# Self attention of a perceiver layer: stacks made by DMA, maxima from high parts, layer norms by row tile

## Chip, core and metric

The kernel runs on one core of one Trainium2 chip. The metric is device time in microseconds: 1697.44 us, the median of three runs (1695.24 to 1698.91).

## What is computed

The layer is cross attention, then self attention with a sparse mixing, then a mixture of experts. Only the self attention is touched. `x` has 512 rows of 512 features, 16 heads of 32 features.

```python
Q = split_heads(jnp.einsum('bsd,od->bso', x, W_Q))
K = split_heads(jnp.einsum('bsd,od->bso', x, W_K))
V = split_heads(jnp.einsum('bsd,od->bso', x, W_V))
Q = layernorm(Q, q_ln_w, q_ln_b)      # over the 32 features of a head
K = layernorm(K, k_ln_w, k_ln_b)
scores = jnp.einsum('bhqd,bhkd->bhqk', Q, K) / jnp.sqrt(jnp.float32(hd))
attn = jax.nn.softmax(scores, axis=-1)
context = jnp.einsum('bhqk,bhkd->bhqd', attn, V)
...
v_weights = sparse_W_V.mean(axis=2)
o_weights = sparse_W_O.mean(axis=1)
```

## The kernel before

All of the program is a sequence of blocks. In a block each engine runs its own list of instructions in order, synchronised by semaphores that are written out by hand, and a block begins on every engine when the one before has ended. The change touches the two blocks `self_projections` and `self_attend`. Constants: `P` 128, `D` and `N` 512, `NT` = `DC` = `G` = `HG` = 4 (row tiles, contraction chunks, groups of heads, heads of a group), `H` 16, `HD` 32, `STK` = `MROW` = 96.

Scores need more precision than one pass gives, so a query or key is held as a high part (rounded to fp32r) and a low part (the rest). A stack has 96 rows a head: for the queries high, high, low, for the keys high, low, high. One matmul over 96 rows then is the sum of three products. `c.stacks` holds the queries, `c.skst` the keys. Two more rows (96 and 97) of `c.stacks` hold the negated row maximum in two parts, against ones in `c.skst`, so that the matmul of 98 rows yields shifted scores for the exponential.

`self_projections`, by engine:

- TensorE (`project`, line 1001) makes all four row tiles of the raw queries in one set of PSUM banks, then all of the keys, each tile being four fp32 matmuls (eight records in the trace). `turn` (L1013) transposes the normalised tiles. The value products come last and reuse the banks of the keys.
- VectorE first sums the mixing weights (L1074, L1076), then centres (L1046 to L1050), sums the squares (L1054), scales (L1058), always over four tiles at once (128x2048), splits into high and low (L1068, L1070) and copies the high part to one place of the stack (L512).
- ScalarE squares (L1102), takes the root (L1106), applies the affine part of the layer norm out of PSUM (L1114), copies the low part to one place (L510) and the values to SBUF (L1123).
- SyncE issues four DMAs a stack for the third place (L508). One call of `stack_copies` is four operations, one for each head of a group, of 32 partitions by 2048 elements (256 KB).
- GpSimd fills the rows of ones and builds the mixing matrices.

`self_attend`: TensorE makes for head after head and row tile after row tile the scores of a query tile against all keys (`whole`, L1190) in one of two PSUM banks, VectorE takes their maximum over the row (L1278), and `whole(i)` waits for the maximum of `i - 2`. After four tiles VectorE negates and splits the maxima (L1282 to L1285), TensorE turns them into rows (`turn`, L1200), ScalarE copies these into the stack (L1249). This runs 20 tiles (`LEAD`) ahead. Then the loop: `scores` (L1208) makes transposed scores in one of three banks, ScalarE takes the exponential (L1258), and after four of them `weighted` adds values (L1219) and denominators (L1223) into the banks `o` and `den`. These two banks are shared by all groups: at the first round of a group TensorE waits for `s_out`, that is for VectorE's `normalise` of the group before (a reciprocal, L1271, and a product, L1273), which VectorE does behind the maxima of a head:

```python
                if h % HG == 2 and h // HG >= 2:
                    normalise(h // HG - 2)
```

The block after, `sparse_mix`, reads all of the normalised result `c.aoT`.

Of the kernel before, what the change touches and what calls it, by code (L numbers as in the profile page):

```python
# [20 lines left out]
P = 128  # L21
# [932 lines left out]
def self_projections(nc, c):  # L954


    with ExitStack() as stack:
        sb, pb, sem = allocators(nc, stack, "sp")
        vm = sb("vm", [P, H])
        om = sb("om", [P, HD])  # L960
        total = sb("total", [P, NT * H])
        mean = sb("mean", [P, NT * H])
        spread = sb("spread", [P, NT * H])
        std = sb("std", [P, NT * H])
        rstd = sb("rstd", [P, NT * H])
        cen = sb("cen", [P, NT, D])
        nrm = sb("nrm", [P, NT, D])
        full = sb("full", [P, G, N])
        hi = sb("hi", [P, G, N], F32R)
        lo = sb("lo", [P, G, N], F32R)  # L970
        queries = pb("queries", [P, NT, D])
        keys = pb("keys", [P, NT, D])
        turned = queries[:, :, :]
        s_raw, s_cen, s_sq, s_var, s_std, s_nrm, s_tp, s_full, s_hi, s_lo, s_v, s_val, s_ones = (
            sem(n) for n in ("raw", "cen", "sq", "var", "std", "nrm", "tp", "full", "hi", "lo", "v", "val", "ones"))
        s_copy_act, s_copy_dve, s_copy_dma = sem("copy_act"), sem("copy_dve"), sem("copy_dma")
        s_step = sem("step")
        s_vm, s_om, s_bv, s_bo = (sem(n) for n in ("vm", "om", "bv", "bo"))
# [3 lines left out]
        KINDS = ((c.stacks, 1, 2, 0), (c.skst, 2, 1, 2))  # L982

        def heads(ap):
            return ap.rearrange("p t (h d) -> p (t h) d", d=HD)

        def wide(ap):
            return ap[:, :].unsqueeze(2).broadcast_to([P, NT * H, HD])

        @block.sync  # L990
        def _(sp):
            for n, (stacks, second_hi, _, _) in enumerate(KINDS):
                sp.wait_ge(s_hi, G * (n + 1))
                stack_copies(sp, stacks, f32(hi[:, :, :]), second_hi, s_copy_dma)
            sp.wait_ge(s_copy_dma, 16 * 2 * HG)

        @block.tensor
        def _(pe):
            def project(out, w, t):
                for k in range(DC):  # L1000
                    mm = pe.matmul(out[:, t, :], c.hT[:, k, t * P:(t + 1) * P], w[:, k, :],
                                   start=(k == 0), stop=(k == DC - 1))
                return mm

            def turn(n):

                pe.wait_ge(s_nrm, n + 1)
                if n:

                    pe.wait_ge(s_full, G)  # L1010
                for g in range(G):
                    for t in range(NT):
                        mm = pe.transpose(turned[:, g, t * P:(t + 1) * P], nrm[:, t, g * P:(g + 1) * P], c.ident[:, :])  # L1013
                    mm.then_inc(s_tp, 1)

            pe.wait_ge(c.sq_in, 16)
            for t in range(NT):
                mm = project(queries, c.swqT, t)
            mm.then_inc(s_raw, 1)
            pe.wait_ge(c.sk_in, 16)  # L1020
            for t in range(NT):
                mm = project(keys, c.swkT, t)
            mm.then_inc(s_raw, 1)
            turn(0)
            pe.wait_ge(c.sv_in, 16)

            pe.wait_ge(s_cen, 2)
            for t in range(NT):
                if t == NT // 2:
                    turn(1)  # L1030
                project(keys, c.swvT, t).then_inc(s_v, 1)

        @block.vector
        def _(dve):
            steps = 0

            def step(instruction):

                nonlocal steps
                steps += 1  # L1040
                instruction.then_inc(s_step, 1)
                dve.wait_ge(s_step, steps)

            def centre(n, raw):
                dve.wait_ge(s_raw, n + 1)
                step(dve.tensor_reduce(total[:, :], heads(raw[:, :, :]), AX.X, ALU.add))  # L1046
                step(dve.tensor_scalar(mean[:, :], total[:, :], 1.0 / HD, None, ALU.mult))
                if n:
                    dve.wait_ge(s_nrm, n)
                dve.tensor_tensor(heads(cen[:, :, :]), heads(raw[:, :, :]), wide(mean), ALU.subtract).then_inc(s_cen, 1)  # L1050

            def normalise(n):
                dve.wait_ge(s_sq, n + 1)
                step(dve.tensor_reduce(spread[:, :], heads(nrm[:, :, :]), AX.X, ALU.add))  # L1054
                dve.tensor_scalar(std[:, :], spread[:, :], 1.0 / HD, EPS, ALU.mult, ALU.add).then_inc(s_var, 1)
                dve.wait_ge(s_std, n + 1)
                step(dve.reciprocal(rstd[:, :], std[:, :]))
                dve.tensor_tensor(heads(nrm[:, :, :]), heads(cen[:, :, :]), wide(rstd), ALU.mult).then_inc(s_nrm, 1)  # L1058

            def split(n):  # L1060
                if n:

                    dve.wait_ge(s_copy_act, HG)
                    dve.wait_ge(s_copy_dve, HG)
                    dve.wait_ge(s_copy_dma, 16 * HG)
                for g in range(G):
                    dve.wait_ge(s_full, G * n + g + 1)
                    dve.tensor_copy(hi[:, g, :], full[:, g, :]).then_inc(s_hi, 1)  # L1068
                    dve.wait_ge(s_hi, G * n + g + 1)
                    dve.tensor_tensor(lo[:, g, :], full[:, g, :], f32(hi[:, g, :]), ALU.subtract).then_inc(s_lo, 1)  # L1070

            wv, wo = mixing_parts(c)
            dve.wait_ge(c.mix_in, 16 * 5 * HG)
            dve.tensor_reduce(vm[:, :], wv, AX.X, ALU.add).then_inc(s_vm, 1)  # L1074
            for i in range(2):
                dve.tensor_reduce(om[:, HD // 2 * i:HD // 2 * i + HD // 2], wo[i], AX.X, ALU.add).then_inc(s_om, 1)  # L1076
            dve.wait_ge(s_om, 2)
            dve.tensor_scalar(om[:, :], om[:, :], 1.0 / TOPM, None, ALU.mult).then_inc(s_om, 1)
            dve.wait_ge(s_vm, 1)
            dve.wait_ge(s_bv, 1)  # L1080
            for j in range(HG):
                rows = slice(HD * j, HD * j + HD)
                dve.tensor_scalar(c.mix_bv[rows, H * j:H * j + H], vm[rows, :], 1.0 / TOPM, None, ALU.mult).then_inc(s_bv, 1)
            centre(0, queries)
            normalise(0)
            centre(1, keys)
            split(0)
            normalise(1)
            stack_copies(dve, KINDS[0][0], f32(hi[:, :, :]), 0, s_copy_dve)
            split(1)  # L1090
# [842 lines left out]
```

## Time and profile before

| | us |
|---|---|
| median of three runs | 1697.44 |
| the profiled execution | 1702.76 |
| its span | 1701.0 |
| TensorE busy | 1551.6 (91%) |
| VectorE busy | 1197.0 (70%) |
| ScalarE busy | 969.2 (57%) |
| GpSimd busy | 373.7 (22%) |

The two blocks lie between 1177 and 1357 us. A row of the timeline gives start, duration, engine, line, operation, output, inputs, shapes and count of a run of equal instructions, in brackets the idle time of the engine before it and what ended that. Ends of matmuls are modelled, so starts are the better measure on TensorE (PE). The granted clock is a share of 2.4 GHz.

### The profile page before, as it was taken

The numbers are of one execution on the slowest core, as the hardware profiler recorded it, in microseconds if no ns is written. First come the engines' busy times: TensorE is split into PE (matmuls) and PEld (weight loads), VectorE is DVE, ScalarE is ACT, GpSimd is POOL, SyncE is SP. The second block draws the span as 40 slices with busy tenths as digits, with TensorE's granted clock in tenths as the row PEclk, the third lists the DMA queues.
The fourth block names the chain that finished last, engine by engine and source line by source line (L and its number), as shares of the span: only waits on it lengthen the run. The fifth ranks groups of instructions, "written<-read, shape, count | busy, mean of one in ns | idle before, by whom it ended". The sixth has DMA issues, their size and how long they took to land. (4 is left out here: it accounts for less than half of the span.)

```text
span 1701.0 us, 21706 instructions
## 1 busy us (share of the span) xinstructions
PE 1551.6 (91%) x7992; PEld 819.7 (48%) x7992; DVE 1197.0 (70%) x1834; ACT 969.2 (57%) x1167; POOL 373.7 (22%) x141
## 2 busy tenths in 40 slices
PE   6799999999999799999999999998877706899998
PEld 4466666666665333333333333333443203777775
DVE  5777677677677799999999999996866384320002
ACT  3366666666666688888888888881444411111110
POOL 4453654654652105030012001001000000100001
PEclk9899999999999899999999999998968757799999
DMA  4454454453453654565454444443110090379993
GB/s 173 153 194 153 145 187 150 159 186 139 171 185 105 156 125 118 138 172 144 116 137 125 124 116 115 118 99 50 26 25 1 7 395 1 118 275 325 327 330 103
DMA packets 117336, 250.26 MB, mean 147 GB/s; under 512 B 9704, under 2 KB 26088, under 8 KB 112752
## 3 DMA queue, kind: packets, MB, share of 16 engines
q1 hardware_dynamic: 115520, 244.68, 46.0%
q0 software_dynamic: 1280, 4.20, 0.8%
q8 instruction: 64, 1.05, 0.3%
q14 instruction: 40, 0.33, 0.1%
q10 hardware_dynamic: 432, 0.01, 0.0%
HBM read 182.26 MB, written 61.34 MB: 143 GB/s over the span
## 5 line engine op out<-in xcount | busy, mean ns | idle before, releaser
L748 ACT ACTIVATE att_pr<-att_sc 128x1024 f32<-128x1024 f32 x512 | 496.2, 1022 | 75.3 <-PE att_sc L665 75.3
L798 DVE TENSOR_TENSOR att_tot<-att_tot,att_pr 128x2048 f32<-128x2048 f32 x200 | 467.1, 2336 | 22.0 <-ACT att_pr L748 1.8
L491 DVE CUSTOM_DVE_ANT_0 ctx_size<-ctx_tot,ctx_size 128x512 f32<-128x512 f32 x512 | 333.0, 688 | 134.6 <-PE ctx_tot L411 130.9
L462 ACT ACTIVATE ctx_size<-ctx_dif 128x1024 f32<-128x1024 f32 x256 | 262.3, 1025 | 125.7 <-PE ctx_dif L411 125.7
L665 PE MATMUL att_sc<-g_stacks,att_kst 98*128 98x512 f32 x1024 | 309.0, 424 | 1.5 <-DVE g_stacks L589 1.5
L665 PEld LDWEIGHTS att_sc<-g_stacks,att_kst 98*128 98x128 f32 x1024 | 173.9, 189 | 236.7 <-ACT att_pr L748 211.5
L679 PE MATMUL att_o<-att_pr,att_val 128*32 128x512 f32 x2048 | 273.6, 606 | 2.0 <-issue 1.9
L1742 ACT ACTIVATE ex_hidT<-ex_hp,m_b 128x128 f32<-128x128 f32 x120 | 34.3, 368 | 185.2 <-PE ex_hp L1697 185.1
L411 PE MATMUL ctx_dif<-ctx_k_dif,f_q_hi 32*128 32x512 f32 x512 | 129.2, 501 | 10.1 <-DVE ctx_best L491 6.1
L411 PE MATMUL ctx_tot<-ctx_k_sum,f_q_hi 32*128 32x512 f32 x512 | 128.4, 498 | 0.0
L86 PE MATMUL f_proj<-f_wv_hi,g_stacks 128*128 128x512 f32 x320 | 120.8, 420 | 0.0
L86 PE MATMUL f_proj<-g_stacks,f_wk_hi 128*128 128x512 f32 x352 | 119.4, 420 | 0.2 <-DVE f_k_lo L206 0.2
L1697 PEld LDWEIGHTS ex_hp<-ex_xT,m_w 128*128 128x128 f32 x960 | 111.0, 194 | 8.0 <-issue 8.0
L1697 PE MATMUL ex_hp<-ex_xT,m_w 128*128 128x128 f32 x960 | 111.4, 278 | 0.8 <-issue 0.8
L1710 PE MATMUL ex_yp<-m_w,ex_hidT 128*128 128x512 f32 x240 | 105.5, 592 | 0.0
L411 PEld LDWEIGHTS ctx_dif<-ctx_k_dif,f_q_hi 32*128 32x128 f32 x512 | 47.8, 183 | 106.7 <-issue 53.5
L100 POOL TENSOR_TENSOR g_stacks<-f_raw,g_stacks 128x2048 fp32r<-128x2048 f32 x21 | 96.7, 4605 | 1.7
L679 PEld LDWEIGHTS att_o<-att_pr,att_val 128*32 128x32 f32 x2048 | 40.4, 108 | 96.8 <-issue 95.4
L593 POOL TENSOR_TENSOR o_aoT<-att_whole,att_rs 128x512 f32<-128x512 f32 x3 | 9.4, 3139 | 330.2 <-DVE att_rs L805 330.2
L1750 DVE COPY ex_xT<-ex_tx 128x512 f32<-128x512 f32 x15 | 10.4, 692 | 96.0 <-PE ex_tx L1651 90.5
L1756 DVE COPY o_yT<-ex_yp 128x512 f32<-128x512 f32 x15 | 10.4, 690 | 91.4 <-PE ex_yp L1710 91.4
L86 PEld LDWEIGHTS f_proj<-g_stacks,f_wk_hi 128*128 128x128 f32 x352 | 60.2, 189 | 29.2 <-issue 20.1
(269 smaller groups left out, 1974.5 us busy)
## 6 DMA issues: line engine op xcount, KB each, us to landing
m_w<-in_W SPq DMA_DIRECT2D x30, 2048.0 KB, 13.6
att_kst<-keys_scratch SPq DMA_DIRECT2D x192, 256.0 KB, 3.9
f_raw<-in_ctx SPq DMA_DIRECT2D x32, 1024.0 KB, 6.0
keys_scratch<-f_k_hi SPq DMA_DIRECT2D x32, 512.0 KB, 2.8
keys_scratch<-f_k_lo SPq DMA_DIRECT2D x32, 512.0 KB, 3.2
values_scratch<-ctx_v SPq DMA_DIRECT2D x32, 512.0 KB, 3.1
att_val<-values_scratch SPq DMA_DIRECT2D x64, 256.0 KB, 2.6
rows_scratch<-mix_blank SPq DMA_DIRECT2D x1, 3840.0 KB, 26.0
```

What stands on the lines that cost most here:

```text
L86: mm = pe.matmul(out, left, right, start=(n == 0), stop=(n == 3 * len(a) - 1))
L100: pool.tensor_tensor(c.lo[b], raw[:, :, :], f32(c.hi[b]), ALU.subtract).then_inc(c.s_lo, 1)
L411: mm = pe.matmul(out[:, r * CH:(r + 1) * CH], c.q_hi[rows, g, t * P:(t + 1) * P], keys[m % 2][rows, g, :], start=True, stop=True)
L462: act.activation(size[:, i % ABS, :], dif[:, :], ACT.Abs).then_inc(s_size, 1)
L491: dve.tensor_tensor_reduce(out=size[:, i % ABS, r * CH:(r + 1) * CH], in0=tot[i % 2][:, r * CH:(r + 1) * CH], in1=size[:, i % ABS, r * CH: ...
L665: mm = pe.matmul(sc[pair % PAIRS][:, r * N:(r + 1) * N], kst[m % CHUNKS][:, j, at:at + P], c.stacks[0:STK + 2, HG * (T // PER_G) + j, :], ...
L679: mm = pe.matmul(o[at, :], val[m % CHUNKS][:, T % KT, at], pr[:, T % SLOTS, j, :], start=first, stop=False, skip_group_check=True)
L748: act.activation(pr[:, T % SLOTS, 2 * s:2 * s + 2, :], sc[(2 * T + s) % PAIRS][:, :].rearrange("p (j q) -> p j q", j=2), ACT.Exp, scale=SC ...
L798: dve.tensor_tensor(tot[b % 2][:, :, :], so_far, pr[:, T % SLOTS, :, :], ALU.add).then_inc(s_add, 1)
L1697: mm = pe.matmul(hp[tau % 2][:, f, :], w1[b][:, k, f * P:(f + 1) * P], xT[tau % 2][:, k, :], start=(k == 0), stop=(k == DC - 1))
L1710: mm = pe.matmul(yp[tau % 2][:, :], hidT[tau % 2][:, f, :], w2[b][:, f, :], start=(f == 0), stop=(f == FC - 1))
L1742: act.activation(hidT[tau % 2][:, f, :], hp[tau % 2][:, f, :], ACT.Relu, bias=b1[:, f, :]).then_inc(s_hid, 1)
```

## The change

The mixing sums go from VectorE at the head of `self_projections` to GpSimd in `self_attend`, as a chain of halvings (`add_up`). The projections run by row tile: eight PSUM banks take the eight raw tiles, all of the layer norm works on one tile (128x512), and ScalarE writes the high part by one affine operation and the full value by a second; GpSimd subtracts them (VectorE for the last tile). Only the first value tile is made there. All three places of both stacks are filled by DMAs from SyncE, 24 in all, those of the keys issued in the second block. `self_attend` takes the maxima from a product of the high parts alone (32 rows), with one row of shift instead of two. The three other value tiles are made in the lead in twelve pieces, and TensorE waits for all DMAs before the first `scores`. The banks `o` and `den` of a group are copied to SBUF (`take`), TensorE waits for that copy, and the normalising is done in four pieces of 128 columns, one behind the maxima of each later head.

The diff, cut to its core:

```diff
+def add_up(pool, out, src, room, s_add, done):
+    half = src.shape[-1] // 2
+    pool.tensor_tensor(room[:, :, 0:half], src[:, :, 0:half], src[:, :, half:], ALU.add).then_inc(s_add, 1)
+    while half > 1:
+        half, done = half // 2, done + 1
+        pool.wait_ge(s_add, done)
+        dst = room[:, :, 0:half] if half > 1 else out.unsqueeze(2)
+        pool.tensor_tensor(dst, room[:, :, 0:half], room[:, :, half:2 * half], ALU.add).then_inc(s_add, 1)
+    return done + 1
...
 def self_projections(nc, c):
...
+            sp.wait_ge(s_hi, NT)
+            for place in (0, 1):
+                stack_copies(sp, c.stacks, f32(hi[0][:, :, :]), place, c.s_copy)
+            sp.wait_ge(s_lo, NT)
+            stack_copies(sp, c.stacks, f32(lo[0]), 2, c.s_copy)
...
+            for n in range(TILES):
+                if n == NT:
+                    pe.wait_ge(c.sk_in, 16)
+                project(raw[n], c.swkT if n >= NT else c.swqT, n % NT).then_inc(s_raw, 1)
+                if n >= 2:
+                    turn(n - 2)
...
+            project(raw[0], c.swvT, 0).then_inc(s_v, 1)
+            turn(TILES - 2)
+            turn(TILES - 1)
...
+            centre(0)
+            for n in range(1, TILES):
+                spreads(n - 1)
+                centre(n)
+                scale(n - 1)
+            spreads(TILES - 1)
+            scale(TILES - 1)
...
+            for n in range(TILES):
                 if n:
+                    root(n - 1)
+                square(n)
+                if n >= 2:
+                    affine(n - 2)
...
+            for n in range(TILES - 1):
...
+                pool.tensor_tensor(lo[kind][:, :, at], full[:, n % 2, :, :], f32(hi[kind][:, :, at]), ALU.subtract).then_inc(s_lo, 1)
...
 def self_attend(nc, c):
...
+            for place in (0, 2):
+                stack_copies(sp, c.skst, f32(hi[1][:, :, :]), place, c.s_copy)
+            stack_copies(sp, c.skst, f32(lo[1]), 1, c.s_copy)
+            sp.wait_ge(c.s_copy, 16 * 2 * 3 * HG)
...
-                pe.matmul(full[i % 2][:, :], c.stacks[0:STK, h, t * P:(t + 1) * P], c.skst[0:STK, h, :],
+                pe.matmul(full[i % 2][:, :], hi[0][at, g, t * P:(t + 1) * P], hi[1][at, g, :],
                           start=True, stop=True).then_inc(s_full, 1)
...
-                    pe.wait_ge(s_out, g)
+                    pe.wait_ge(s_take, 2 * g)
...
             for i in range(LEAD):
                 whole(i)
...
                 if i % NT == NT - 1 and i > NT:
                     turn(i // NT - 1)
+                if 1 <= i <= DC * (NT - 1):
+                    value_product(i - 1)
+            pe.wait_ge(s_val, NT - 1)
+            pe.wait_ge(c.s_copy, 16 * 2 * 3 * HG)
...
+                dve.reciprocal(rs[:, at], total).then_inc(s_rs, 1)
+                dve.wait_ge(s_rs, PIECES * g + piece + 1)
+                dve.tensor_tensor(c.aoT[:, g, at], values, rs[:, at], ALU.mult).then_inc(s_out, 1)
+
+            def take(g):
+
                 dve.wait_ge(s_pv, NT * (g + 1))
                 if g >= 1:
...
+                for n, bank in enumerate((den, o)):
+                    dve.tensor_copy(held[:, n, :], bank[:, :]).then_inc(s_take, 1)
+
+            later = [(g, piece) for g in range(G) for piece in range(PIECES)]
             for h in range(H):
                 for i in range(NT * h, NT * h + NT):
                     dve.wait_ge(s_full, i + 1)
                     dve.tensor_reduce(c.neg[:, h, i % NT:i % NT + 1], full[i % 2][:, :], AX.X, ALU.max).then_inc(s_max, 1)
+                    if i % STEPS == HG * 2 and i // STEPS >= 2:
+                        take(i // STEPS - 2)
...
+                if h >= 2 * HG + 2:
+                    normalise(*later.pop(0))
+            while later[0][0] < G - 2:
+                normalise(*later.pop(0))
+            take(G - 2)
+            for g, piece in later:
+                normalise(g, piece)
```

## Rows read from the trace of the kernel before

**Rows 1.** windows: span, busy time and count of each engine, PEclk, DMA share, GB/s

```profile
1177.00:1242.00 65.00, 49.95 (x128) 23.18 (x128) 45.41 (x46) 27.23 (x24) 8.89 (x8) 0.87 0.25 46
1242.00:1260.40 18.40, 15.97 (x37) 9.02 (x37) 15.16 (x37) 2.39 (x5) 0.00 (x0) 0.50 0.00 0
1260.40:1352.50 92.10, 78.61 (x411) 33.61 (x411) 44.79 (x83) 43.52 (x77) 0.00 (x0) 0.85 0.00 1
```

**Rows 2.** timeline of TensorE, projections and the first score matmul

```profile
1177.26 16.84 PE L1001 MATMUL sp_queries<-a_swqT,g_hT 128*128 128x512 f32 x32 [1.11 <-PEq L542]
...
1193.93 13.90 PE L1001 MATMUL sp_keys<-a_swkT,g_hT 128*128 128x512 f32 x32
...
1207.66 1.91 PE L1013 MATMUL sp_queries<-g_ident,sp_nrm 128*128 128x128 f32 x16
...
1212.85 8.80 PE L1001 MATMUL sp_keys<-a_swvT,g_hT 128*128 128x512 f32 x16 [3.28 <-DVE sp_cen L1050]
...
1242.29 1.22 PE L1190 MATMUL sa_full<-a_skst,g_stacks 96*128 96x512 f32 x2 [10.82 <-DVE sa_shift L1265]
```

**Rows 3.** groups of VectorE, both blocks: busy, mean ns, idle before

```profile
L1278 DVE TENSOR_REDUCE g_neg<-sa_full 128x1 f32<-128x512 f32 x64 | 41.5, 686 | 26.2 <-PE sa_full L1190 25.7
...
L1271 DVE RECIPROCAL sa_rs<-sa_den 128x512 f32<-128x512 f32 x4 | 13.4, 3354 | 23.1 <-PE sa_den L1223 23.1
...
L1070 DVE TENSOR_TENSOR sp_lo<-sp_full,sp_hi 128x512 fp32r<-128x512 f32 x8 | 5.5, 692 | 0.3
...
L512 DVE CAST a_skst<-sp_hi 32x2048 fp32r<-32x2048 f32 x4 | 4.9, 1214 | 0.1
...
L1282 DVE TENSOR_SCALAR sa_shift_hi<-g_neg 128x4 fp32r<-128x4 f32 x16 | 2.7, 170 | 0.6
```

**Rows 4.** timeline of ScalarE, projections

```profile
1208.36 2.78 ACT L1114 ACTIVATE sp_full<-sp_queries,a_aff 128x512 f32<-128x512 f32 x4 [4.61 <-PE sp_queries L1013]
...
1232.71 7.71 ACT L510 ACTIVATE a_skst<-sp_lo 32x2048 fp32r<-32x2048 f32 x4 [1.53 <-DVE sp_lo L1070]
...
1240.44 1.08 ACT L1123 ACTIVATE a_sval<-sp_keys 128x512 f32<-128x512 f32 x2
```

**Rows 5.** groups of GpSimd, whole span

```profile
L100 POOL TENSOR_TENSOR g_stacks<-f_raw,g_stacks 128x2048 fp32r<-128x2048 f32 x21 | 96.7, 4605 | 1.7
```

**Rows 6.** timelines of GpSimd and VectorE in the context projections

```profile
72.71 4.59 POOL L100 TENSOR_TENSOR f_third<-f_raw,f_third 128x2048 fp32r<-128x2048 f32 x1
...
73.11 4.74 DVE L480 TENSOR_TENSOR ctx_k_dif<-f_k_hi 128x512 fp32r<-128x512 f32 x1
```

**Rows 7.** timeline of SyncE's queue, a stack's four DMAs

```profile
1216.25 3.44 SPq L508 DMA_DIRECT2D g_stacks<-sp_hi  x4
```

**Rows 8.** windows, two microseconds while they move

```profile
1219.00:1221.00 2.00, 2.00 (x6) 0.87 (x5) 1.61 (x4) 1.57 (x2) 0.00 (x0) 1.00 0.96 221
```

**Rows 9.** the tile sp_hi: its DMAs from issue to landing

```profile
DMA to landing us min/median/max: 3.1/4.3/5.4
```

**Rows 10.** timeline of TensorE, rounds of the loop

```profile
1279.06 0.50 PE L1190 MATMUL sa_full<-a_skst,g_stacks 96*128 96x512 f32 x1
...
1283.90 0.50 PE L1190 MATMUL sa_full<-a_skst,g_stacks 96*128 96x512 f32 x1
...
1291.62 1.93 PE L1219 MATMUL sa_o<-sa_pr,a_sval 128*32 128x512 f32 x8 [4.66 <-DVE o_aoT L1273]
...
1295.19 0.70 PE L1190 MATMUL sa_full<-a_skst,g_stacks 96*128 96x512 f32 x1
...
1330.13 0.96 PE L1208 MATMUL sa_sc<-g_stacks,a_skst 98*128 98x512 f32 x3
...
1333.66 0.96 PE L1208 MATMUL sa_sc<-g_stacks,a_skst 98*128 98x512 f32 x3
...
1341.60 2.34 PE L1208 MATMUL sa_sc<-g_stacks,a_skst 98*128 98x512 f32 x4
...
1347.18 0.96 PE L1208 MATMUL sa_sc<-g_stacks,a_skst 98*128 98x512 f32 x3
```

More of the change, by code:

```diff
@@ L954, in self_projections @@
 def self_projections(nc, c):
+    TILES = 2 * NT
     with ExitStack() as stack:
         sb, pb, sem = allocators(nc, stack, "sp")
[L959 to L976, printed above, removed]
@@ L977, in self_projections @@
-        s_step = sem("step")
-        s_vm, s_om, s_bv, s_bo = (sem(n) for n in ("vm", "om", "bv", "bo"))
+        total = sb("total", [P, TILES, H])
+        mean = sb("mean", [P, 2, H])
+        spread = sb("spread", [P, 2, H])
+        std = sb("std", [P, 2, H])
+        rstd = sb("rstd", [P, 2, H])
+        cen = sb("cen", [P, 3, D])
+        sq = sb("sq", [P, D])
+        full = sb("full", [P, 2, G, P])
+        hi, lo = c.own_hi, c.own_lo
+        raw = [pb(f"raw{n}", [P, D]) for n in range(TILES)]
@@ L979, in self_projections @@
+        s_raw, s_total, s_mean, s_cen, s_sq, s_spread, s_var, s_std, s_rstd, s_nrm, s_tp, s_full, s_hi, s_lo, s_v, s_ones = (
+            sem(n) for n in ("raw", "total", "mean", "cen", "sq", "spread", "var", "std", "rstd", "nrm", "tp", "full", "hi",
+                             "lo", "v", "ones"))
+        s_last, s_val = sem("last"), sem("val")
         nc.clear_and_free_semaphores(c.spent)
         block = stack.enter_context(nc.Block())
-        KINDS = ((c.stacks, 1, 2, 0), (c.skst, 2, 1, 2))
@@ L1033, in _ @@
+            pe.wait_ge(c.sv_in, 16)
+            pe.wait_ge(s_hi, 1)
+            pe.wait_ge(s_full, 1)
+            project(raw[0], c.swvT, 0).then_inc(s_v, 1)
+            turn(TILES - 2)
+            turn(TILES - 1)
         @block.vector
         def _(dve):
[L1035 to L1044, printed above, removed]
-                dve.wait_ge(s_raw, n + 1)
[L1046 to L1055, printed above, removed]
-                dve.wait_ge(s_std, n + 1)
[L1057 to L1090, printed above, removed]
-            stack_copies(dve, KINDS[1][0], f32(hi[:, :, :]), 0, s_copy_dve)
@@ new lines, in centre @@
+            def centre(n):
+                dve.wait_ge(s_raw, n + 1)
+                dve.tensor_reduce(total[:, n, :], heads(raw[n][:, :]), AX.X, ALU.add).then_inc(s_total, 1)
+                dve.wait_ge(s_total, n + 1)
+                dve.tensor_scalar(mean[:, n % 2, :], total[:, n, :], 1.0 / HD, None, ALU.mult).then_inc(s_mean, 1)
+                if n >= 3:
+                    dve.wait_ge(s_tp, n - 2)
+                dve.wait_ge(s_mean, n + 1)
+                dve.tensor_tensor(heads(cen[:, n % 3, :]), heads(raw[n][:, :]), wide(mean[:, n % 2, :]),
+                                  ALU.subtract).then_inc(s_cen, 1)
```

239 lines of the change are left out of this document (135 added, 104 removed).

## The prediction, made blind

> **What bounds the kernel now.** The windows view cuts the two self attention blocks into stages [rows 1]: 65.0 us for the projections, 18.4 us for a lead of maxima, 92.1 us for the loop. TensorE is busy for 50.0, 16.0 and 78.6 us of these, so only the loop is TensorE's, and the lead runs at a granted clock of 0.50, the lower of the two levels (1.2 GHz). The timeline of TensorE names the holes. In the projections the query tiles take 16.84 us, the key tiles 13.90 us, sixteen transposes 1.91 us; TensorE waits 3.28 us for VectorE before the values, and sits idle for 10.82 us before the first score matmul at 1242.29 [rows 2]. That hole is VectorE (four copies of 1214 ns after the splits [rows 3]) and ScalarE (four copies in 7.71 us, then two value tiles to 1241.5), which build the stacks [rows 4]. So VectorE and ScalarE in turn set the projection stage, and the work is in blocks of four tiles, so that little overlaps. The lead is set by VectorE's 686 ns maxima [rows 3]. In the loop one round of four scores takes 4.84 us (1279.06 to 1283.90), but the round in which a group of heads ends takes 11.29 us (1283.90 to 1295.19), of which 4.66 us is TensorE's wait for VectorE to normalise [rows 10]. All behind it (sparse mixing, routing, experts) waits for the block to end, so what is saved here comes off the end.
>
> **The change, part by part.** Positions are in the profiled execution of before: span 1701.0 us, measured 1702.76 us, 0.3% over the median of 1697.44. I sum differences and subtract them from the median.
>
> *Projections by row tile.* One projection of a tile is eight matmul records of 13.90/32 = 0.434 us, 3.43 us with overlap. The 16.84 us of the queries is 2.96 us over that, the slow clock at the start, which stays [rows 2]. TensorE then does 8 x 3.43 + 2.96 = 30.4 us and, between them, five turns of four transposes at 1.91/16 = 0.12 us, 0.5 us each: the last raw tile is there at 1177.26 + 33.0 = 1210.2. VectorE does per tile two reductions, two tensor products of 0.69 us (the row of 128x512 [rows 3]) and three small ones of 0.17: 3.4 us with gaps, under TensorE's 3.93. ScalarE does a square and two affines, 2.78/4 = 0.70 us each, and a small root [rows 4]: 2.4 us. GpSimd's low part is a quarter of 4605 ns, 1.15 us [rows 5]. Tail behind 1210.2: VectorE centres the last tile (1.75), scales the one before (0.95), sums the squares (0.9), waits for the root (0.7) and scales (0.95), 5.3 us; turn 0.6; ScalarE still has the affines of tile 6 and a value tile, so its last affine ends at 7.7; the last low part 0.8. That is 8.5 us, 1218.7. V product and turn 6 lie under it. The mixing sums (three reductions) leave VectorE's head of the queue at no gain, since they ended before the first queries were there.
>
> *Who queues behind what.* VectorE now issues in order spreads, centre, scale, with a wait for ScalarE in each; the waiting instruction blocks the next tile's centring, and that blocks ScalarE's square. GpSimd's low part of a tile falls at the start of the next tile but two, where VectorE does its small mean operation. The trace shows such a meeting: VectorE's 128x512 tensor_tensor beside GpSimd's took 4.74 us, starting 0.4 us after it, both ending within 0.6 us of each other [rows 6]. So each meeting can cost up to 1.15 us. VectorE has 0.5 us of slack per tile; I take 1.0 us in all, bounds 0 and 8 x 1.15 = 9 us. Stage end 1219.7, and with 0.8 us between blocks (ScalarE's last value, 1240.44 + 1.08, to 1242.29, as now [rows 2, 4]) the first score matmul at 1220.5. Gain over 1242.29: 21.8 us.
>
> The Trainium skill (SBUF — State Buffer, "Who interferes with whom") says that a VectorE operation with two SBUF inputs, or a copy or tensor_scalar in a two-port mode, and a GpSimd operation exclude each other for the whole instruction. The trace agrees (4.74 us for what alone takes 0.69). The rule speaks against moving the splits and sums to GpSimd. By it every meeting is charged in full, which is the first rival below; the row by itself leaves open whether the small operations meet it.
>
> *Stacks by DMA.* Removed: eight copies on VectorE and eight on ScalarE (4.9 and 7.7 us a stack [rows 3, 4]), which were the hole before 1242.29, already counted. Added: 24 DMAs of 256 KB on SP's queue instead of 8. Four are issued in 3.44 us [rows 7], and at a DMA share of 0.96 the engines move 221 GB/s [rows 8], 1.18 us for 256 KB. Query stacks: first issue when four high parts are ready, near 1203.5, twelve take 14.2 + 1.7 us, to 1219.4. Key stacks start with the second block, 1219.7, end 1235.6. Who waits: TensorE before the first score of the loop, near 1243. Cover 7 us; cost nothing. SP issues nothing else until the expert weights, in the next block.
>
> *The lead.* TensorE no longer waits for stacks. Each of twelve steps has a 32-row matmul (0.21 us for 512 columns at 2.4 GHz; the trace has no 32-row one here, its nearest are three 98-row ones in 0.96 us [rows 10] and two 96-row ones in 1.22 us at half clock [rows 2], the bounds) and one piece of a value product, 0.86 us: 1.07 us, more than VectorE's 0.69, so 12.9 us, two turns 1.0. TensorE's clock: after the 3.28 us gap of before sixteen records took 8.80 instead of 6.87 us [rows 2], 1.9 us lost; the gap here is some 4 us, and I take 2.5 us (bounds 0, and 12.9 if the clock never rises). Then six more steps at 0.72, a turn, the row copy, 6.3 us with the wait. Sum 22.7 us against 18.1 (1242.29 to 1260.40 [rows 1, 2]). First score at 1243.2: gain 17.2 us. The shorter shift (one row for two, one small operation of 170 ns for three) saves VectorE 0.33 us a head, under TensorE. GpSimd's mixing sums: 3 x 2032 elements per partition at 4605/2048 ns [rows 5] is 13.7 us, with overheads 18 us, free until VectorE's first normalisation (some 25 us into the loop). They may hold VectorE's small operation once a head: 0 to 2.3 us each, taken in the bounds.
>
> *The loop.* Its rounds stay as they are: the same number of matmuls, and the pace of the two full banks. What goes is the wait for normalising. Excess now: 6.45 us (11.29 - 4.84) at each of the first two boundaries (the second repeats the first), 4.41 us at the third (7.94, 1333.66 to 1341.60, against 3.53, 1330.13 to 1333.66), and 2.05 us of slow clock in the round behind that (5.58, to 1347.18) [rows 10]: 19.4 us. What comes: two copies of a bank, 0.65 us each (the reduction's row; a copy out of PSUM is of the same shape). The first two pairs stand behind the first maximum of a head, so the maximum after next is 1.3 us late and TensorE's fourth score matmul with it: 1.3 us twice. The third pair lies in VectorE's idle time, under four scores. The normalising pieces (reciprocal 3354/4 = 0.84 us [rows 3] and product 0.2, 1.1 us) go behind each head's maxima: 3.0 + 0.2 + 1.1 = 4.3 us of VectorE in 4.84. Late next is nothing. The slow first round gives back 0.5 us. Loop 92.1 - 19.4 + 2.6 - 0.5 = 74.8 us, a gain of 17.3. The last normalisation in four pieces is 4.7 instead of 4.1 us: +0.6.
>
> *Sum.* 17.2 (projections and lead together) + 17.3 - 0.6 = 33.9 us; 1697.4 - 33.9 = 1663.5.
>
> **Rivals.**
> 1. *VectorE and GpSimd exclude each other.* For: [rows 6]. Against: the two meet only for small operations, with 0.5 us slack. Full price: 8 x 1.15 in the projections, some 3 in the lead: +12, 1675.
> 2. *TensorE's clock stays at 1.2 GHz through the lead.* For: the lead of before has 0.50 throughout [rows 1], with TensorE 16.0 of 18.4 us in use by the modelled ends. Against: value products fill it without gaps, and products of that kind brought the clock up at 1177: 2.96 us lost are seven slow records [rows 2]. Price 12.9 - 2.5 = +10, 1673.
> 3. *Copying the banks out does not take the wait away.* TensorE's values still wait for VectorE behind its maxima; if the copies came behind a whole head (2.6 us) each boundary would keep 4 to 5 us: +9, 1672. Against: they stand behind one maximum in the program.
> 4. *Slower than before: the stacks' DMAs don't overlap.* TensorE waits for all 24 before any score. At 4.3 us (the median landing time now [rows 9]) one behind the other they would end at 1203.5 + 103 = 1307, 64 us behind the lead's end: 1663.5 + 64 = 1727. It decides for slower from (1243.2 + 33.9 - 1203.5)/24 = 3.1 us a DMA. Against: while each took 4.3 us to land, the engines moved 221 GB/s, which is 1.18 us apiece, so they do overlap [rows 8, 9].
> 5. *More than forecast:* no meeting on VectorE, the clock comes back at once, the tail is a microsecond shorter: 1657.
>
> **How the numbers follow.** Forecast 0.62, rival 1 0.12, rival 2 0.09, rival 3 0.04, rival 4 0.03, rival 5 0.10. The forecast's own range is 1659 to 1669 (the turns, the tail and the pace of the lead, each a microsecond or two). For 8 in 10 with the bounds of both unknown costs I reach to rival 5 below, and above to where rivals 1 to 3 hold in full: 1655 to 1675. Under 0.2% (3.4 us) can't be told from no change; only rival 4, cut short, would end there. Faster 0.96, same 0.01, slower 0.03.
>
> **What would show it.** The first 32-row score matmul some 43 us after the first query product (now 65); nrm tiles on VectorE every 3.9 us, and no VectorE operation of over 1 us in that stretch (longer ones mean rival 1); the granted clock in the lead near 0.9 (0.50 means rival 2); TensorE's wait for the stacks absent (present means rival 4); rounds of 4.84 us and no wait of over 1.5 us at the boundaries (longer means rival 3). A loop round other than 4.84 us would prove wrong that the rounds keep their pace.

## The result, and the profile after

Over 20 runs each the changed kernel took 1716.88 us in the median (1704.06 to 1727.58) and the kernel before 1698.58 us (1694.41 to 1704.53) beside it: the ratio of the means is 1.0096, with a 95% interval of 1.0079 to 1.0112. The change makes the kernel 1% slower, where 2% faster was forecast. The profiled run took 1711.86 us with a span of 1710.0 us; that of before was 1702.76 and 1701.0. The profiled run of the changed kernel is 5 us below its median and that of before 4 us above its own, so the traces show 9 us of difference where the medians have 18; the rest lies in runs that no trace shows.

The windows view of the changed kernel, cut at the same three events as [rows 1] (columns as there):

```profile
1178.19:1222.63 44.44, 38.50 (x104) 17.62 (x105) 31.30 (x57) 17.39 (x33) 16.04 (x9) 0.92 0.44 81
1222.63:1262.40 39.77, 38.32 (x61) 13.38 (x62) 15.61 (x27) 4.19 (x8) 19.81 (x33) 0.59 0.45 89
1262.40:1360.10 97.70, 95.69 (x411) 36.32 (x411) 49.30 (x85) 44.95 (x77) 0.00 (x0) 0.81 0.00 1
```

The projections went from 65.0 to 44.4 us, almost as forecast (43.2). But the lead is 39.8 us where 22.7 stood in the forecast, and the loop 97.7 where 74.8 stood. In both TensorE is now busy nearly without a hole, 95.69 of 97.70 us in the loop, for 411 records as before: it hardly waits for anybody, the same matmuls take it longer, and its clock is lower than the 1.00 of full speed (0.59 and 0.81). Against the forecast the three stages are +1.2, +17.1 and +22.9 us, the first query product is 0.9 us later, and the last normalising to the next block's first copy 0.8 us longer than before (0.6 forecast). That is 42.3 of the 43.0 us between 1668.9 (1702.76 - 33.9) and 1711.86.

The timeline of TensorE and its weight loads (PEld) in the changed kernel, once in the lead and once in the loop at full clock:

```profile
1231.20 0.28 PEld L1185 LDWEIGHTS sa_full<-a_own_hi 32*128 32x128 f32 x1 [1.50 <-issue]
1231.20 0.79 PE L1185 MATMUL sa_full<-a_own_hi 32*128 32x512 f32 x1
1231.92 0.50 PEld L1173 LDWEIGHTS sa_sc<-a_swvT,g_hT 128*128 128x128 f32 x2 [0.44 <-issue]
1231.92 2.08 PE L1173 MATMUL sa_sc<-a_swvT,g_hT 128*128 128x512 f32 x2
1233.93 0.28 PEld L1185 LDWEIGHTS sa_full<-a_own_hi 32*128 32x128 f32 x1 [1.50 <-issue]
...
1314.20 0.49 PE L1185 MATMUL sa_full<-a_own_hi 32*128 32x512 f32 x1
1314.62 0.19 PEld L1203 LDWEIGHTS sa_sc<-g_stacks,a_skst 97*128 97x128 f32 x1 [0.24 <-issue]
1314.62 0.49 PE L1203 MATMUL sa_sc<-g_stacks,a_skst 97*128 97x512 f32 x1
1315.05 0.18 PEld L1185 LDWEIGHTS sa_full<-a_own_hi 32*128 32x128 f32 x1 [0.24 <-issue]
1315.05 0.50 PE L1185 MATMUL sa_full<-a_own_hi 32*128 32x512 f32 x1
...
1319.89 0.18 PEld L1185 LDWEIGHTS sa_full<-a_own_hi 32*128 32x128 f32 x1 [0.84 <-issue]
```

Two things are to be seen. Each weight load begins at the same moment as its own matmul's record, when the one before it has ended, and not under that one: 0.18 to 0.19 us at full clock and 0.28 at half clock stand open at every change between a 32-row matmul and a taller one. And a step of the lead is 2.73 us (1231.20 to 1233.93), a round of the loop at full clock 5.69 us (1314.20 to 1319.89) where it was 4.84 [rows 10].

### The profile page after: what moved, and what is told of

Read it like the earlier page. It is cut to its first block and busy times, and to the rows that moved or that the text cites. A ratio compares the mean times of both kernels' runs of the same rounds, so it can differ in the third digit from the quotient of the medians.

```text
span 1710.0 us, 21807 instructions
## 1 busy us (share of the span) xinstructions
PE 1582.6 (93%) x7992; PEld 821.7 (48%) x7992; DVE 1187.6 (69%) x1843; ACT 963.2 (56%) x1179; POOL 400.8 (23%) x174
## 5 line engine op out<-in xcount | busy, mean ns | idle before, releaser
L798 DVE TENSOR_TENSOR att_tot<-att_tot,att_pr 128x2048 f32<-128x2048 f32 x200 | 467.2, 2336 | 21.8 <-ACT att_pr L748 1.6
L1330 DVE TENSOR_REDUCE g_neg<-sa_full 128x1 f32<-128x512 f32 x64 | 43.7, 691 | 60.1 <-PE sa_full L1185 59.7
```

Source lines behind the costliest of these rows:

```text
L798: dve.tensor_tensor(tot[b % 2][:, :, :], so_far, pr[:, T % SLOTS, :, :], ALU.add).then_inc(s_add, 1)
L1330: dve.tensor_reduce(c.neg[:, h, i % NT:i % NT + 1], full[i % 2][:, :], AX.X, ALU.max).then_inc(s_max, 1)
```

## What the theories were

The experiments below name four theories. Theory S: a 32-row matmul beside 97-row or 128-row ones stops TensorE at each change, and the clock stays low behind it. The rivals named ahead of the first runs were P (the value products, DMAs or GpSimd's sums that lie beside the lead make it slow) and O (another reason); L came with it as a variant, that few rows at work hold the clock down, stops or not.

## Experiments

**The maxima without 32-row matmuls (no32).** The kernel after, with the lead's product over 128 rows of queries padded with zeros, and the loop's over 96 rows of the stacks as before.

```diff
+            for h in range(HG + 1):
+                at = slice(HD * (h % HG), HD * (h % HG) + HD)
+                sp.dma_start(f32(c.padded[at, h, :]), f32(hi[0][at, h // HG, :])).then_inc(c.s_pad, 16)
...
+                if i >= LEAD:
+                    pe.matmul(full[i % 2][:, :], c.stacks[0:STK, h, t * P:(t + 1) * P], c.skst[0:STK, h, :],
+                              start=True, stop=True).then_inc(s_full, 1)
+                    return
-                pe.matmul(full[i % 2][:, :], hi[0][at, g, t * P:(t + 1) * P], hi[1][at, g, :],
+                pe.matmul(full[i % 2][:, :], c.padded[:, h, t * P:(t + 1) * P], hi[1][:, g, :],
```

> Theory S (a matmul of 32 rows beside one of 97 or 128 rows can't have its weights loaded under its neighbour, and the stops that this makes leave TensorE's clock at its lower level): the maxima of the lead are taken with 128 rows (the queries of a head padded with zeros), those of the loop with 96 rows of the stacks, so no matmul of 32 rows is left. Lead 39.8 to 23-25 us, loop 97.7 to 75-77 us, granted clock near 0.9 in both, span about 1670 us. Theory P (the lead is slow by the value products, or by what DMAs and GpSimd do under it): the lead stays near 39 us at a clock of 0.5, only the loop falls, span about 1687 us. Theory O (neither: the 512 columns cost more for another reason): span stays near 1710 us.

Measured: 1670.79 us, ratio to before 0.983 (0.979 to 0.987). The windows of its lead and its loop:

```profile
1224.66:1246.55 21.89, 20.48 (x62) 11.22 (x62) 14.50 (x27) 4.19 (x8) 19.38 (x31) 0.90 0.92 181
1246.55:1319.10 72.55, 68.42 (x411) 30.00 (x411) 47.58 (x85) 43.37 (x77) 0.61 (x2) 1.00 0.00 1
```

Lead 21.9 us (22.7 forecast), loop 72.6 us (74.8 forecast), both 1 to 3 us shorter than theory S expected; granted clock 1.00 in the loop. All else of the change is in this kernel, the value products, the DMAs and GpSimd's sums among it, so P falls, and both lost terms of the forecast are back. Its timeline in the loop:

```profile
1290.14 0.19 PEld L1192 LDWEIGHTS sa_full<-a_skst,g_stacks 96*128 96x128 f32 x1 [0.52 <-DVE g_neg L1341]
1290.14 0.50 PE L1192 MATMUL sa_full<-a_skst,g_stacks 96*128 96x512 f32 x1
1290.25 0.19 PEld L1213 LDWEIGHTS sa_sc<-g_stacks,a_skst 97*128 97x128 f32 x1
1290.48 0.39 PE L1213 MATMUL sa_sc<-g_stacks,a_skst 97*128 97x512 f32 x1
1291.93 0.51 PE L1192 MATMUL sa_full<-a_skst,g_stacks 96*128 96x512 f32 x1 [1.06 <-DVE g_neg L1341]
...
1294.89 0.19 PEld L1192 LDWEIGHTS sa_full<-a_skst,g_stacks 96*128 96x128 f32 x1 [0.84 <-issue]
1294.90 0.50 PE L1192 MATMUL sa_full<-a_skst,g_stacks 96*128 96x512 f32 x1
```

Between 96 and 97 rows there is no stop: the load of L1213 begins 0.11 us after the matmul before it and lies under it. The load at 1294.89 does stand open, as its like does in the kernel before (1283.90): it follows the matmuls of the values and denominators, whose weights have 32 columns (128*32). So the first of a round's eight changes cost its stop already. That leaves seven new stops of 0.21 us, 1.5 us a round. An ordinary round of no32 takes 4.84 us (1284.02 to 1288.86) and has waits for VectorE's maxima in it, which take up some 0.6 us of the 1.5: 4.84 becomes 5.69. The round printed here has the two copies of a bank in it, with 1.06 us of such waiting; it takes 6.04 us (1288.86 to 1294.90), and its like in the changed kernel 6.18 (1300.72 to 1306.90).

**The same in the loop alone (loop96).** The lead keeps its 32-row matmuls; the diff is the `if i >= LEAD` branch above.

> The lead as in the changed kernel (32 rows), the maxima of the loop from 96 rows of the stacks. Theory S: the lead stays at 39-40 us with a clock of 0.5, the loop falls from 97.7 to 75-79 us, span 1688-1692 us. Theory O: no change, 1710 us. If the low clock of the lead is carried into the loop for long, the loop stays over 85 us and the span over 1697 us.

Measured: 1686.61 us, ratio 0.992 (0.989 to 0.994); lead 40.9 us at a clock of 0.54, loop 74.4 us. So both places count. From no32 to this kernel the median rises by 15.8 us (in the traces +19.0 in the lead, +1.9 in the loop, -3.5 in the projections, whose last DMAs for the padding are gone). From here to the changed kernel the loop is 23.3 us longer in the traces and the median 30.3 us higher, where single runs of the changed kernel lie up to 24 us apart.

**The value products in a run ahead of the maxima (values_first).**

```diff
+            for n in range(DC * (NT - 1)):
+                value_product(n)
             for i in range(LEAD):
...
-                if 1 <= i <= DC * (NT - 1):
-                    value_product(i - 1)
```

> The twelve pieces of value products stand in one run ahead of the maxima of the lead; all maxima keep 32 rows. Theory S: one change of rows in the lead instead of 24: products 12-14 us, twenty maxima at VectorE's pace 14-16 us, lead 28-31 us instead of 39.8, loop unchanged at 95-100 us, span 1699-1702 us. Theory L (few rows at work, not the stops, hold the clock down): the maxima run of the lead is at a clock of 0.5 and the lead is 30-33 us. Theory P: products at 1.7 us each again, lead over 36 us.

Measured: 1702.30 us, ratio 1.002 (1.000 to 1.004). The products take 13 us, the maxima behind them 19.6 us, and the loop 97.8 us as in the changed kernel:

```profile
1236.12:1255.72 19.60, 17.18 (x39) 8.55 (x38) 14.14 (x25) 4.19 (x8) 7.96 (x18) 0.56 0.20 40
1255.72:1353.49 97.77, 95.72 (x412) 36.36 (x411) 49.49 (x85) 44.94 (x77) 0.00 (x0) 0.81 0.00 1
```

The changes of height between maxima and value products are gone and the lead is 7.2 us shorter (32.6 for 39.8). But among 32-row maxima alone the granted clock falls from 1.00 (1236.12 to 1238) to 0.50 (from 1239 on), though products of full height had brought it up just before. That is a first sign for L and no more: the 96-row maxima of the kernel before, which wait for VectorE too, ran at 0.50 as well [rows 1], and in the changed kernel the last eight maxima of the lead, of 32 rows and with no value product between them, ran at nearly full clock:

```profile
1255.00:1262.40 7.40, 5.95 (x19) 2.63 (x19) 5.79 (x11) 1.81 (x4) 0.00 (x0) 0.96 0.00 0
```

**The kernel before with 32-row maxima and nothing else (before32).**

```diff
-                pe.matmul(full[i % 2][:, :], c.stacks[0:STK, h, t * P:(t + 1) * P], c.skst[0:STK, h, :],
+                pe.matmul(full[i % 2][:, :], c.stacks[0:HD, h, t * P:(t + 1) * P], c.skst[0:HD, h, :],
```

> The kernel before with one edit: the maxima come from the first 32 rows of the stacks instead of 96 (the high parts alone), in lead and loop. Theory S: lead unchanged near 18 us (only the transposes have other rows), each of eleven loop rounds 0.8-0.9 us longer at full clock (4.84 to 5.7) and more where the clock drops, loop 92.1 to 102-115 us, span 1711-1724 us. Theory P or O: within 3 us of the kernel before, 1701 us.

Measured: 1725.23 us, ratio 1.016 (1.012 to 1.020). The windows:

```profile
1241.27:1260.90 19.63, 17.73 (x37) 8.25 (x37) 14.81 (x35) 2.39 (x5) 0.00 (x0) 0.50 0.00 0
1260.90:1374.80 113.90, 101.26 (x412) 37.71 (x411) 46.83 (x83) 44.87 (x77) 0.00 (x0) 0.74 0.00 1
```

One line in the kernel before costs 21.8 us of the loop (92.1 to 113.9), nearly the 22.9 us that the forecast of the loop was wrong by. The lead, which was at half clock and paced by VectorE already, loses only 1.5 (19.6 for 18.1). The median is 24.9 us higher. The cause needs no other part of the change.

**Stops without few-row work (tiny32).** A 32-row matmul of only 32 columns ahead of each full-height maxima product of no32.

```diff
+                pe.matmul(full[i % 2][:, 0:32], hi[0][0:HD, 0, 0:P], hi[1][0:HD, 0, 0:32], start=True, stop=True)
```

> The kernel with 128-row maxima in the lead and 96-row maxima in the loop, with one small matmul of 32 rows and 32 moving columns ahead of each of the 64 maxima's products; its result is written over by that product, so nothing of the computation changes. It tells the stops beside a 32-row matmul apart from the few rows of work that such a matmul gives the array. The 32 columns are a sixteenth of a product's 512, at most 0.05 us each of their own, 3 us in all. If the cost comes from changing between 32-row and full-height matmuls (theory S), each of the 64 steps again has a weight load that isn't covered before and after the small one: the lead is again near 40 us instead of 21.9, the loop near 98 us instead of 72.6, at a granted clock of 0.50 in the lead, and the time 1710 to 1735 us. If the cause is that 512 columns go through only 32 rows and that this holds the clock down (theory L), almost all columns here go through 96 to 128 rows and the time is 1671 to 1678 us.

Measured: 1691.42 us, ratio 0.995 (0.993 to 0.996), between the two expectations.

```profile
1224.72:1254.18 29.46, 29.14 (x82) 14.58 (x82) 15.11 (x26) 4.18 (x8) 19.92 (x33) 0.87 0.69 135
1254.18:1337.96 83.78, 81.45 (x454) 37.33 (x454) 49.52 (x85) 44.66 (x77) 0.00 (x0) 0.98 0.00 1
```

```profile
1236.31 0.18 PEld L1191 LDWEIGHTS sa_full<-a_own_hi 32*128 32x128 f32 x1 [0.76 <-DVE g_neg L1342]
1236.52 0.19 PEld L1196 LDWEIGHTS sa_full<-a_own_hi,a_padded 128*128 128x128 f32 x1
1236.52 0.50 PE L1196 MATMUL sa_full<-a_own_hi,a_padded 128*128 128x512 f32 x1
1237.80 0.28 PE L1191 MATMUL sa_full<-a_own_hi 32*128 32x32 f32 x1
```

The loads of both matmuls stand open, and a step is 1.49 us for the 1.10 us of no32 (1232.17 to 1233.27 there). A loop round is 5.80 us. But the granted clock is 0.87 in the lead and 0.98 in the loop. So the stops, with the small matmul's own time, cost 7.6 us in the lead (29.5 for 21.9) and 11.2 us in the loop (83.8 for 72.6), and they don't hold the clock down; they let it rise later (0.55 from 1229 to 1233, where no32 has 0.99), which is a part of the 7.6. What is left to the changed kernel, 10.3 and 13.9 us, comes with a clock of 0.59 for 0.87 and 0.81 for 0.98. Theory S was right on the stops and wrong on the clock.

**64 rows (rows64).**

```diff
-                    pe.matmul(full[i % 2][:, :], c.stacks[0:STK, h, t * P:(t + 1) * P], c.skst[0:STK, h, :],
+                    pe.matmul(full[i % 2][:, :], c.stacks[0:2 * HD, h, t * P:(t + 1) * P], c.skst[0:2 * HD, h, :],
...
-                pe.matmul(full[i % 2][:, :], c.padded[:, h, t * P:(t + 1) * P], hi[1][:, g, :],
+                half = slice(64 * (j // 2), 64 * (j // 2) + 64)
+                pe.matmul(full[i % 2][:, :], c.padded[half, h, t * P:(t + 1) * P], hi[1][half, g, :],
```

> The same kernel with all 64 maxima's products over 64 rows: in the lead 64 rows of the padded queries against 64 rows of the keys' high parts, in the loop the first 64 rows of the stacks. In the loop the maxima are then taken over the high parts and one of the two low-part terms, over 96 rows before; the set-off of a row may differ in its last bits and no more. If only matmuls over a part of the array's height (32 or 64 rows) beside full ones cost the stops (theory S), this one pays them as the changed kernel does: lead near 40 us, loop near 98 us, 1700 to 1720 us. If the rows at work decide (theory L), 64 rows stand half way: 1680 to 1695 us. If 64 rows cost nothing, 1671 us, and the cost belongs to 32 rows alone.

Measured: 1695.76 us, ratio 0.998 (0.996 to 0.999).

```profile
1221.09:1248.86 27.77, 26.59 (x62) 10.23 (x62) 17.72 (x26) 4.18 (x8) 19.92 (x33) 0.87 0.72 141
1248.86:1340.87 92.01, 90.01 (x412) 34.98 (x411) 49.52 (x85) 44.93 (x77) 0.00 (x0) 0.86 0.00 1
```

At full clock its rounds are 5.69 us (1274.93 to 1280.62), the pace of the 32-row kernel: 64 rows stop like 32. The lead has tiny32's clock (0.87) and is 1.7 us shorter: there 64 rows do not hold the clock down. In the loop the clock is 0.86, between the 0.98 of tiny32 and the 0.81 of the 32-row kernel, and the loop is 8.2 us longer than tiny32's at the same number of stops. The time is just above what L expected (1680 to 1695) and below what S did (1700 to 1720). So the cause has two halves: the stops, and a lower clock where 512 columns go through only 32 rows, and in the loop through 64.

**GpSimd's low part behind the small operation (mean_first)**, on top of no32. GpSimd's subtraction of a tile is made to wait for VectorE's small mean operation, which it stood beside:

```diff
+                pool.wait_ge(s_mean, min(n + 4, TILES))
```

> The kernel with 128-row and 96-row maxima, and GpSimd's subtraction of a low part made to wait until VectorE's small mean operation of four tiles later is done, so that the two no longer stand side by side. Where they met, that operation of 16 elements took 1.21 us in the changed kernel against 0.17 us alone, once in each of the later tiles. If the two engines shut each other out (the rival that the prediction priced at 1.0 us for the stage), the operation is back at 0.17 us, the period of a tile falls from 4.32 to about 3.9 us for the four or five tiles concerned, and the first score matmul comes 1 to 2 us sooner; it doesn't come 4 us sooner because SyncE, which issues the padding's and the stacks' DMAs, ends the stage. Time 1669 to 1670 us against 1670.8. If the long operation had another cause, it stays at 1.2 us and the time at 1670.8 us or over.

Measured: 1669.18 us, ratio 0.981 (0.979 to 0.983); by its time it can't be told from no32, so the traces have to show it. The timelines of VectorE and GpSimd in the changed kernel:

```profile
1204.40 1.27 POOL L1126 TENSOR_TENSOR a_own_pr<-sp_full,a_own_hi 128x512 f32<-128x512 f32 x1 [3.06 <-ACT sp_full L1099]
...
1204.49 1.21 DVE L1051 TENSOR_SCALAR sp_mean<-sp_total 128x16 f32<-128x16 f32 x1
1205.81 0.69 DVE L1055 TENSOR_TENSOR sp_cen<-sp_raw,sp_mean 128x512 f32<-128x512 f32 x1
...
1210.12 0.69 DVE L1055 TENSOR_TENSOR sp_cen<-sp_raw,sp_mean 128x512 f32<-128x512 f32 x1
```

and in mean_first:

```profile
1204.11 1.27 POOL L1133 TENSOR_TENSOR a_own_pr<-sp_full,a_own_hi 128x512 f32<-128x512 f32 x1 [2.60 <-DVE sp_mean L1055]
...
1203.76 0.17 DVE L1055 TENSOR_SCALAR sp_mean<-sp_total 128x16 f32<-128x16 f32 x1
1204.04 0.69 DVE L1059 TENSOR_TENSOR sp_cen<-sp_raw,sp_mean 128x512 f32<-128x512 f32 x1
1204.65 0.24 DVE L1064 RECIPROCAL sp_rstd<-sp_std 128x16 f32<-128x16 f32 x1
1204.92 0.99 DVE L1066 TENSOR_TENSOR sp_cen<-sp_cen,sp_rstd 128x512 f32<-128x512 f32 x1
1207.91 0.69 DVE L1059 TENSOR_TENSOR sp_cen<-sp_raw,sp_mean 128x512 f32<-128x512 f32 x1
```

The operation of 16 elements is back from 1.21 to 0.17 us and the period of a tile from 4.31 to 3.87 us, and the first score matmul comes 45.5 us after the first query product for 47.3 in no32. The exclusion is shown, and its price in the stage is 1.8 us. (In the changed kernel a second form of it stands at the very end of the stage: the last scaling, L1062 at 1217.62, both inputs in SBUF, took 1.55 us instead of 0.69 beside GpSimd's operation of 1217.36.) It is also shown that not every operation is shut out: the product of a tensor in PSUM with one operand in SBUF (L1059, at 1204.04) ran 0.69 us beside GpSimd's, while the one with both in SBUF (L1066) took 0.99 instead of 0.69 us and ended 0.5 us behind GpSimd's (1205.38).

**Fewer DMAs issued at the end of the stage (best)**, on top of mean_first: the query stacks' low parts are issued at the start of the next block.

```diff
-            sp.wait_ge(s_lo, NT)
-            stack_copies(sp, c.stacks, f32(lo[0]), 2, c.s_copy)
...
+            stack_copies(sp, c.stacks, f32(lo[0]), 2, c.s_copy)
             for place in (0, 2):
```

> As the one before, and the four DMAs of the query stacks' low parts are issued in the next stage, behind the keys' first eight, instead of at the end of the projections. SyncE spent 4.05 us on them as the last thing before the stage ended. The first score matmul should come 1.5 to 4 us sooner than in the kernel with 128-row and 96-row maxima (47.3 us after the first query product there, 43.5 to 45.8 here), with VectorE as what ends the stage; the DMAs then end some 2 to 4 us later after the start of the lead, against a lead of 21.9 us that they lie beside. Time 1667 to 1669 us. If the stacks are then late, the loop's first matmul waits for DMAs and the gain is lost.

Measured: 1668.35 us, ratio 0.980 (0.978 to 0.982), the fastest version here, but its interval and that of mean_first overlap. The first score matmul stands 43.2 us after the first query product, 4.1 us sooner than in no32 and 2.3 us sooner than in mean_first, the lead is 1.4 us longer (23.3) and the loop the same. (The four DMAs went ahead of the keys' eight, not behind them as the expectation says; the sum is not touched by that.)

**The output banks not copied out (no_copies)**, on top of no32: the part on the output banks undone.

```diff
-                    pe.wait_ge(s_take, 2 * g)
+                    pe.wait_ge(s_out, g)
...
-                    if i % STEPS == HG * 2 and i // STEPS >= 2:
-                        take(i // STEPS - 2)
...
-                if h >= 2 * HG + 2:
-                    normalise(*later.pop(0))
+                if h % HG == 2 and h // HG >= 2:
+                    normalise(h // HG - 2)
```

> The kernel with 128-row and 96-row maxima, with the part on the output banks undone: no bank is copied out, a group of heads is normalised whole by one reciprocal of 128x512 and one product, as in the kernel before, and TensorE's values wait for that. It measures the term of the sum for the loop by itself. If that term is right (19.4 us of excess at the ends of the groups less 2.6 us for the copies, 0.5 us for a slow first round), the waits of some 4.7 us come back at two ends of groups and a shorter one at the third, the loop is 86 to 90 us instead of 72.6, the slow clock behind the waits is back, and the time is 1684 to 1688 us. If the copies had only moved the wait (rival 3 of the prediction), the loop stays within 4 us of 72.6 and the time is 1675 us or less.

Measured: 1682.11 us, ratio 0.991 (0.987 to 0.994). A window of its loop, its wait at the end of a group, and the same place in the changed kernel (TensorE, then VectorE):

```profile
1246.74:1333.66 86.92, 73.54 (x411) 31.42 (x411) 42.05 (x61) 43.31 (x77) 0.49 (x2) 0.92 0.00 1
```

```profile
1275.96 1.94 PE L1224 MATMUL sa_o<-a_own_pr,a_sval 128*32 128x512 f32 x8 [4.41 <-DVE o_aoT L1320]
```

```profile
1303.78 0.50 PE L1185 MATMUL sa_full<-a_own_hi 32*128 32x512 f32 x1 [0.43 <-DVE g_neg L1330]
...
1301.85 0.68 DVE L1324 COPY sa_held<-sa_den 128x512 f32<-128x512 f32 x1
1302.45 0.68 DVE L1324 COPY sa_held<-sa_o 128x512 f32<-128x512 f32 x1
```

The loop is 14.4 us longer than with the copies (86.9 for 72.6); 16.8 was the forecast of this part (19.4 - 2.6). The waits of 4.4 us are back and, at 0.92, some slow clock behind them. Rival 3 is refuted by this. The whole time rises by 11.3 us, 2 us less than the least that was expected, so the part is worth having by itself.

## Why the prediction was wrong, point by point

- *The projections: right.* 44.4 us for 43.2. The order of the terms held: VectorE ends the stage in the changed kernel. The meetings with GpSimd were taken at 1.0 us; taking them away in mean_first gave 1.8. The rule of the Trainium skill cited there (SBUF — State Buffer, "Who interferes with whom") is borne out by mean_first, for the operation with two SBUF inputs and for a small tensor_scalar too. Rival 1's full price, 12 us, was too high: the mean operation took 1.2 us in four tiles and 0.57 in one, and of its 1.04 us VectorE's slack took more than half (the period went from 3.87 to 4.31). But its ground against, that the two meet only for small operations, was wrong: the last scaling met GpSimd too.
- *The stacks by DMA: right.* TensorE's first score of the loop waits for ScalarE's row and not for a DMA. The issues end at 1234.3 in the changed kernel, and the last four land a median of 7.5 us after issue, some 20 us ahead of that score. Rival 4 is refuted.
- *The lead: the step that failed.* "Each of twelve steps has a 32-row matmul (0.21 us ...): 1.07 us." With full-height matmuls a step was 1.09 us at full clock and 2.13 at half (in mean_first, 1228.83 to 1229.92 and 1224.28 to 1226.41). With 32 rows it was 2.73, all at half clock: 0.6 us a step for stops (7.2 us) and, 1.04 us a step less the 2.5 us allowed, 10 us for the clock. Together 17.2 us, where 17.1 were missed. Rival 2 named the clock, and its row, 0.50 in the lead of before, was a sign; but its ground against, that full-height products between would bring the clock up, holds where the maxima aren't of 32 rows (0.90 in no32, 0.87 in rows64) and not where they are (0.59). Its price, 10 us, left the stops out, and so did the bounds of the term: both came from rows of 96 and 98 rows among their like.
- *The loop: the step that failed.* "Its rounds stay as they are: the same number of matmuls, and the pace of the two full banks." The count stayed, the height didn't. At full clock a round is 5.69 us, not 4.84: of the eleven rounds with maxima, nine lose 0.85 us each at that clock and the two with copies hardly any, some 8 us in all. The other 15 of the 22.9 us missed go with the lower clock, under which the stops are longer too. (Against no32 the loop lost 25.1 us, which tiny32 parts into 11.2 and 13.9.) The prediction's own test, that a round other than 4.84 us proves the pace wrong, is what happened.
- *The ends of the groups: right.* The waits of 4.66 us [rows 10] are 0.43 us in the changed kernel, less than the 1.3 us taken.

The evidence was in the trace of before. The prediction says that it has no 32-row matmul "here" and takes 0.21 us by the columns. But the context's scores are such matmuls, and the timeline of TensorE there, in the kernel before, reads:

```profile
98.75 0.62 PE L86 MATMUL f_proj<-g_stacks,f_wk_hi 128*128 128x512 f32 x2
99.21 0.40 PE L86 MATMUL f_proj<-g_stacks,f_wk_lo 128*128 128x512 f32 x1
99.53 0.18 PEld L411 LDWEIGHTS ctx_dif<-ctx_k_dif,f_q_hi 32*128 32x128 f32 x2 [0.37 <-issue]
99.53 0.50 PE L411 MATMUL ctx_dif<-ctx_k_dif,f_q_hi 32*128 32x512 f32 x2
99.54 0.50 PE L411 MATMUL ctx_tot<-ctx_k_sum,f_q_hi 32*128 32x512 f32 x2
99.97 0.30 PEld L86 LDWEIGHTS f_proj<-g_stacks,f_wk_hi 128*128 128x128 f32 x2 [0.25 <-issue]
```

From 99.53 to 99.97 is 0.44 us for four matmuls of 512 columns over 32 rows that run at once, where full-height ones follow each other every 0.23 us (two from 98.75 to 99.21), and the loads on both sides stand open. At two changes for each maximum, 0.2 us each, the twelve steps of the lead would have had 24 x 0.2 = 4.8 us of stops. The loop has seven new ones in each of eleven rounds, 77 x 0.2 = 15.4 us, less the slack of VectorE's maxima (0.6 us a round, as the runs show it, 7 us): 13 us in all, and the forecast would have been near 1677 us. The loss by the clock, 24 us, could not have been read there, since those matmuls run four at once and the clock of that stretch is 1.00.

The Trainium skill (TensorEngine Tiling (Array Packing), "Key Properties") says that a change of the tiling mode drains TensorE. The runs agree: matmuls over 32 and 64 rows beside 96 to 128 stop, 96, 97 and 128 among one another don't. The page gives no price for a change. Here a stop was 0.2 us at 2.4 GHz and 0.3 us at 1.2 GHz.

What stays open is why the clock stays low. The runs show that it goes with 512-column matmuls over 32 rows, and in the loop over 64, not with the stops (tiny32) and not with zeros in the rows (the lead of no32 has three quarters of its query rows zero and is at 0.90). It isn't strict either: the changed kernel's clock was 0.50 for the first 32 us of its lead, 0.96 in the last 7 us, 0.50 for the first 16 us of its loop, and rose and fell again behind that, with 32-row maxima in all of these stretches. A lead in which 32-row maxima of four heads run at once, as the context's do, was not tried; it needs four banks where the maxima have two.

## What to carry to other kernels

Count a matmul's height as well as its columns: fewer rows saved TensorE no time here, and between taller neighbours each 32-row or 64-row matmul added two weight loads that nothing hid. Before such a form is brought in, look anywhere in the trace for rows of that form beside the other one, with their weight loads. A sum that is right for its other parts can still have the wrong sign. Here padding the operand with zeros by five DMAs, and one line for the loop, turned +1% into -2%.

## What the runs showed of the hardware

- A matmul over 32 or 64 rows next to one over 96 to 128 had its weight load in the open, and so had its neighbour: 0.18 to 0.19 us at full clock, 0.28 to 0.29 at half. A change between weights of 32 columns (128*32) and of 128 did the same (1293.04 and 1294.89 in no32, 1282.04 and 1283.90 in the kernel before).
- An operation of 16 elements on VectorE took 1.21 us instead of 0.17 because GpSimd was in a 1.27 us tensor_tensor. A tensor_tensor with one operand in PSUM ran beside it unhindered.
- With 32-row maxima the granted clock was 0.50 (1.2 GHz) through the first 32 us of the lead, in which TensorE was busy without a hole. So being busy by the records did not bring the upper level there. The window of the changed kernel:

```profile
1222.60:1255.00 32.40, 32.37 (x43) 10.78 (x43) 9.82 (x16) 2.38 (x4) 19.84 (x33) 0.50 0.55 109
```
